# Inverse square roots of a two-stage convolution kernel: GpSimd's power in place of ScalarE seeds and VectorE Newton steps

## The reference

```
x = x + L0(gn(x), mask)                       # x: 8 x 64 x 16 x 16, fp32
x = x + L1(gn(x), weight, alphas, betas, bias)
gn: 32 groups of 2 channels: (g - mean(g)) / sqrt(var(g) + 1e-5)

L0, contextual attention, per image (f = gn(x)):
  fd = f[:, ::2, ::2]                         # 8 x 8 positions
  w  = 3x3 patches of fd;  wn = w / max(|w|, 1e-4)
  yi = <patches of fd, wn>                    # 64 x 64 cosines
  yi = fuse(fuse(yi) turned) turned back      # two 3-tap diagonal sums
  yi = softmax(10 * yi * mm, over patches) * mm   # mm: patches clear of the mask
  out = transposed conv of yi with 4x4 patches of f / 4
L1: 3x3 convolution 64 -> 64; its weight is w*a / (1 + exp(w*b)) in 4 x 4 blocks, plus bias
```

## Time and profile before

| | |
|---|---|
| Time, median of 3 runs | 55.9 us (55.76 to 56.01) |
| Span of the profiled execution | 53.4 us, first to last instruction |
| Time around that span | 55.9 - 53.4 = 2.5 us (the profiled execution has no separate time but its span) |
| PE busy | 39.2 us, 73%, 502 matmuls |
| DVE busy | 34.8 us, 65%, 143 instructions |
| ACT busy | 16.0 us, 30%, 50 instructions |
| POOL busy | 19.5 us, 37%, 49 instructions |
| ACT, the Ln of the group norms | 4 instructions, mean 204 ns |
| DMA | 2.37 MB, mean 44 GB/s |

### The profile page before, as it was taken

How to read it: one execution, slowest core, us unless ns; L and a number is a source line. 1 busy time by engine, 2 the same in 40 slices (tenths; PEclk the granted TensorE clock), 3 DMA queues, 4 the chain that set the end, 5 groups by cost and what they waited for, 6 DMA issues and landing times.

```text
span 53.4 us, 1316 instructions
## 1 busy us (share of the span) xinstructions
PE 39.2 (73%) x502; PEld 25.6 (48%) x502; DVE 34.8 (65%) x143; ACT 16.0 (30%) x50; POOL 19.5 (37%) x49
## 2 busy tenths in 40 slices
PE   1996757996999988999589908999999999000000
PEld 0331242673389876986369704444468886000000
DVE  3907799769896889999999999959990200300000
ACT  4500304666752352726798420004300000000000
POOL 5994887979999600203006960000000000000000
PEclk9999999999999999999999999999999999999555
DMA  0399996000000000000000000000000111111110
GB/s 0 88 370 228 310 184 140 5 0 0 18 0 0 0 0 0 12 0 0 0 12 0 0 0 0 0 0 0 0 0 18 37 42 48 49 48 49 48 49 18
DMA packets 2335, 2.37 MB, mean 44 GB/s; under 512 B 281, under 2 KB 2201, under 8 KB 2330
## 3 DMA queue, kind: packets, MB, share of 16 engines
q1 hardware_dynamic: 1770, 1.96, 14.3%
q10 hardware_dynamic: 560, 0.33, 2.0%
HBM read 1.77 MB, written 0.52 MB: 43 GB/s over the span
## 4 chain that ended last, share of the span: by engine, by line
DVE 42%; PE 30%; DMA 6%; issue 3%; ACT 3%; DVEq 0%
PE bank L583 12%; PE bank L595 12%; DMA xh<-x_in_dram 6%; DVE gn_stats L674 4%; DVE wrec L761 3%; PE bank L488 3%; DVE x2h L704 2%; DVE fst L704 2%; DVE ftl L822 2%; DVE pst L807 2%; DVE x L830 2%; DVE xn L704 2%; DVE n2c L774 2%; DVE p L807 1%; DVE gn_mv L678 1%
## 5 line engine op out<-in xcount | busy, mean ns | idle before, releaser
L478 PE MATMUL bank<-idle 128*128 128x512 f16 x27 | 8.7, 455 | 1.1 <-POOL idle L278 1.1
L305 POOL TENSOR_SCALAR fq<-xh,gn_mean,gn_rstd 128x128 f32<-128x128 f32 x8 | 6.7, 852 | 0.2 <-DVE xn L704 0.2
L488 PE MATMUL bank<-fmv,fst 128*64 128x128 f16 x108 | 4.2, 224 | 1.0 <-ACT fmv L381 0.8
L921 DVE SCALAR_TENSOR_TENSOR o_sb<-bank,x1b 128x256 f32<-128x256 f32 x4 | 1.6, 422 | 5.0 <-PE bank L595 5.0
L543 PE MATMUL bank<-k_sb,pst 128*64 128x256 f16 (+2 forms) x72 | 4.3, 262 | 0.8 <-DVE pst L713 0.7
L488 PEld LDWEIGHTS bank<-fmv,fst 128*64 128x64 f16 x108 | 3.3, 108 | 2.8 <-ACT fmv L381 2.8
L478 PEld LDWEIGHTS bank<-idle 128*128 128x128 f16 x27 | 2.7, 116 | 4.2 <-issue 1.8
L337 POOL TENSOR_TENSOR wl<-w,wh 64x288 f16<-64x288 f32 x4 | 2.9, 726 | 3.6 <-ACT wh L457 3.4
L543 PEld LDWEIGHTS bank<-k_sb,pst 128*64 128x64 f16 x72 | 3.3, 109 | 1.5 <-DVE pst L713 0.8
L360 ACT ACTIVATE gn_ln<-gn_var 128x2 f32<-128x2 f32 x4 | 0.8, 204 | 9.6 <-DVE gn_var L687 9.5
L583 PE MATMUL bank<-x2h,wh 128*128 128x512 f16 x9 | 2.4, 388 | 1.6 <-DVE x2h L704 1.6
(11 more groups left out here) (120 smaller groups left out, 90.7 us busy)
## 6 DMA issues: line engine op xcount, KB each, us to landing
xg<-x_in_dram SPq DMA_DIRECT2D x2, 256.0 KB, 6.2
out_dram<-o_sb SPq DMA_DIRECT2D x4, 128.0 KB
k_sb<-k_dram SPq DMA_DIRECT2D x1, 496.0 KB, 5.8
xh<-x_in_dram SPq DMA_DIRECT2D x1, 256.0 KB, 3.2
xh<-x_in_dram ACTq DMA_DIRECT2D x1, 256.0 KB, 3.6
w_sb<-weight_in_dram SPq DMA_DIRECT2D x1, 72.0 KB, 2.9
c_sb<-c_dram ACTq DMA_DIRECT2D x1, 64.0 KB, 3.0
c_sb<-c_dram SPq DMA_DIRECT2D x1, 64.0 KB, 5.9
```

What stands on the lines that cost most here:

```text
L305: pool.tensor_scalar(fq[u][:, j, 2 * q:2 * q + 2, :].rearrange("p s (a b) -> p s a b", a=G), xh[u][:, j, :].rearrange("p (a r b s) -> p r ...
L478: te.matmul(ps, idle[:, 0:P], idle[:, :], start=True, stop=True)
L488: i = te.matmul(gram_ps[u][half(g), :, :], st, mv[:, :, k // 3:k // 3 + G, k % 3:k % 3 + G], start=part_st == part_mv == k == 0, stop=part ...
```

## The change

ScalarE's seeds and VectorE's Newton steps go. In their place GpSimd raises the 128x2 tile to the power -0.5 in one tensor_tensor instruction, with a tile `power` that it fills once. `F_SCALE` and `Y_SCALE` become 1, since the result of the power is used as it is. VectorE then waits for `rstd_ready` or `rnorm_ready` from GpSimd. The six powers are put at fixed places in GpSimd's program.

```diff
-F_SCALE = 16.0
-Y_SCALE = 16.0
+F_SCALE = 1.0
+Y_SCALE = 1.0
...
@@ gpsimd
+            def gn_rstd(i, u):
+                n = norm[i][u]
+                pool.wait_ge(var_ready, UNITS * i + u + 1)
+                pool.tensor_tensor(n.rstd[:, :], n.var[:, :], power[:, :], ALU.pow).then_inc(rstd_ready, 1)
+
+            def inverse_norms(u):
+                pool.wait_ge(n2_ready, u + 1)
+                pool.tensor_tensor(rnorm[u][:, :], n2c[u][:, :], power[:, :], ALU.pow).then_inc(rnorm_ready, 1)
+
             zero([idle], idle_set)
+            link(pool.memset(power[:, :], -0.5))
...
             zero(pst, zeros_p)
+            gn_rstd(0, 0)
             zero([wh, wl], zeros_w)
             pool.wait_ge(mask_in, 16)
...
+            gn_rstd(0, 1)
             pool.wait_ge(xn_ready, 1)
             f_by_parity(0, 0)
+            inverse_norms(0)
...
             for j in range(IPU):
                 f_by_parity(1, j)
+            inverse_norms(1)
             zero(x2h + x2l, zeros_x2)
...
             pool.wait_ge(zeros_x2, 2 * UNITS)
+            gn_rstd(1, 0)
+            pool.wait_ge(rstd_ready, UNITS + 1)
             for g in range(2):
...
+            pool.wait_ge(wl_ready, 4)
+            gn_rstd(1, 1)
@@ scalar
-                link(act.activation(scratch[:, :], v[:, :], ACT.Ln, scale=1.0 / scale ** 2))
-                return act.activation(y[:, :], scratch[:, :], ACT.Exp, scale=-0.5)
...
@@ vector
-            def newton(dst, v, y, a, b, scale):
-
-                link(dve.tensor_tensor(a[:, :], y[:, :], y[:, :], ALU.mult))
-                link(dve.scalar_tensor_tensor(b[:, :], a[:, :], -0.5 / scale ** 2, v[:, :], ALU.mult, ALU.mult))
-                return dve.scalar_tensor_tensor(dst[:, :], b[:, :], 1.5, y[:, :], ALU.add, ALU.mult)
-
             def gn_rstd(i, u):
-                n = norm[i][u]
-                dve.wait_ge(gn_y0, UNITS * i + u + 1)
-                link(newton(n.rstd, n.var, n.y0, n.ya, n.yb, F_SCALE))
+                dve.wait_ge(rstd_ready, UNITS * i + u + 1)
...
             def high_x2(u):
...
+                gn_rstd(1, u)
+                for r in range(2):
+                    copy_x1(u, 1, r)
                 dve.wait_ge(zeros_x2, 2 * UNITS)
```

More of the change, by code:

```diff
@@ L136, in __init__ @@
                 self.var = sb(name + "_var", P, IPU)
[L137 to L140, removed]
                 self.rstd = sb(name + "_rstd", P, IPU)
@@ L150, in build @@
         gdiag = per_unit("gdiag", P, IPU, L)
-        n2, n2c, nln, ny0, nya, nyb, rnorm = (per_unit(t, P, IPU) for t in (
-            "n2", "n2c", "nln", "ny0", "nya", "nyb", "rnorm"))
+        n2, n2c, rnorm = (per_unit(t, P, IPU) for t in ("n2", "n2c", "rnorm"))
+        power = sb("power", P, IPU)
         y32 = per_unit("y32", P, IPU, L)
@@ L189, in build @@
         idle_set = sem("idle_set")
-        pool_step, dve_step, act_step = map(sem, ("pool_step", "dve_step", "act_step"))
+        pool_step, dve_step = map(sem, ("pool_step", "dve_step"))
         mask_row, mask_bc, keep_ready = map(sem, ("mask_row", "mask_bc", "keep_ready"))
@@ L193, in build @@
         wexp_ready, w32_ready, wh_ready, wl_ready = map(sem, ("wexp_ready", "w32_ready", "wh_ready", "wl_ready"))
-        moments, groups, var_ready, mean_ready, gn_y0 = map(sem, (
-            "moments", "groups", "var_ready", "mean_ready", "gn_y0"))
+        moments, groups, var_ready, mean_ready, rstd_ready = map(sem, (
+            "moments", "groups", "var_ready", "mean_ready", "rstd_ready"))
         xn_ready, fh_center, fl_center, fq_ready = map(sem, ("xn_ready", "fh_center", "fl_center", "fq_ready"))
         f_copied = [[sem(f"f_copied{u}{part}") for part in range(2)] for u in range(UNITS)]
-        gram_done, n2_ready, norm_y0, y32_ready, yh_ready, yl_ready = map(sem, (
-            "gram_done", "n2_ready", "norm_y0", "y32_ready", "yh_ready", "yl_ready"))
+        gram_done, n2_ready, y32_ready, yh_ready, yl_ready = map(sem, (
+            "gram_done", "n2_ready", "y32_ready", "yh_ready", "yl_ready"))
         rnorm_ready = sem("rnorm_ready")
@@ L348, in _ @@
             act.dma_start(par_sb[:, :], par).then_inc(par_in, 16)
[L350 to L358, removed]
-                link(act.activation(scratch[:, :], v[:, :], ACT.Ln, scale=1.0 / scale ** 2))
-                return act.activation(y[:, :], scratch[:, :], ACT.Exp, scale=-0.5)
-            def gn_seed(i, u):
-                n = norm[i][u]
-                act.wait_ge(var_ready, UNITS * i + u + 1)
-                seed(n.y0, n.var, n.ln, F_SCALE).then_inc(gn_y0, 1)
             def exp_weight(b):
@@ L386, in weight_alpha @@
                                scale=par_sb[:, b:b + 1]).then_inc(walpha_ready, 1)
-            def norm_seed(u):
-                act.wait_ge(n2_ready, u + 1)
-                seed(ny0[u], n2c[u], nln[u], Y_SCALE / F_SCALE).then_inc(norm_y0, 1)
             def high_y1(u):
@@ L421, in _ @@
             act.wait_ge(zeros_f, 2 * UNITS)
-            gn_seed(0, 0)
             copies_of_f(0, 0)
             copies_of_f(0, 1)
-            gn_seed(0, 1)
             act.wait_ge(w_in, 16)
@@ L430, in _ @@
             copies_of_f(1, 0)
-            norm_seed(0)
             copies_of_f(1, 1)
@@ L438, in _ @@
             high_y1(0)
-            norm_seed(1)
             act.wait_ge(zeros_p, UNITS)
@@ L458, in _ @@
                                    ACT.Copy).then_inc(wh_ready, 1)
-            gn_seed(1, 0)
             high_b(1)
             x1_and_bias(0)
-            gn_seed(1, 1)
             x1_and_bias(1)
@@ L774, in norms @@
                 dve.tensor_scalar(n2c[u][:, :], n2[u][:, :], MIN_NORM2, None, ALU.max).then_inc(n2_ready, 1)
-            def inverse_norms(u):
-                dve.wait_ge(norm_y0, u + 1)
-                newton(rnorm[u], n2c[u], ny0[u], nya[u], nyb[u], Y_SCALE / F_SCALE).then_inc(rnorm_ready, 1)
             def normalise_gram(u):
@@ L868, in _ @@
             low_f(1)
-            inverse_norms(0)
             normalise_gram(0)
@@ L880, in _ @@
             logits(0)
-            inverse_norms(1)
             normalise_gram(1)
```

## The result

The changed kernel takes 57.36 us (57.31 to 57.78, 4 runs) against 55.83 us (55.73 to 56.01, 4 runs): a ratio of 1.0294, interval 1.0255 to 1.0333. It is slower, by 1.5 us. The profiled execution took 57.36 us with a span of 55.5 us.

What follows compares the result with a forecast made beforehand. VectorE's chain, then TensorE's convolution, was taken to bound the kernel. A delay of 2.0 less a gain of 0.6 made the 53.4 us span 54.8; with 2.5 around it, 57.3 us, 8-in-10 range 55.8 to 61.8.

Steps and rivals of the forecast that it cites:

- Scale costs nothing: F and Y at scale 1 change constants and no instruction, so they cost 0.
- c = 0.6: What one power costs GpSimd's queue, from release to hand-over: 0.6 us, between ends of 0.3 and 0.84.
- the delay: Unit 1's patch norms: the power, queued behind other GpSimd work, ends at 21.27, so yh(1) starts 2.0 us later.
- Hidden powers: Powers for unit 0's first group norm and patch norms finish while VectorE is busy, so VectorE does not wait.
- Second norm, unit 0, 1.3 at x2h: Without the slow Newton steps, the x2h pair ends at 30.8 instead of 32.07, 1.3 us gained for the convolution's start.
- The second wait, 0.6 kept: VectorE's x2 pair meets wl, TensorE waits for unit 1's statistics, and 0.6 of the 1.3 us gained stays.
- Second norm, unit 1, at 0: Its power waits for wl, two copies cover most of it, and TensorE still has unit 0's matmuls: cost 0.
- The end moves one for one with the convolution's start: TensorE is busy 13.15 of 13.20 us from 32.20, so the end follows the convolution's start unless a wait opens.
- 2.5 us around the span: The median lies 2.5 us above the profiled span, and the same distance was assumed after the change.
- GpSimd's queue without a gap: Sign: GpSimd's queue runs without idle from 6.1 us until the second rnorm at about 21.3.
- The slow power: Rival: a power computed element by element in software may take 2 us or more, giving 64.3 us; chance 0.15.
- the draw: Rival: a power costs 0.3 us and the gain is near 0.9, giving 55.8 us; chance 0.08.

Runs made afterwards that it cites:

- e1: The kernel before with F_SCALE and Y_SCALE at 1 and nothing else changed: 55.78 us, ratio 0.9994.
- e4: The changed kernel with a multiply of the tile `power` by itself in place of each power, same queue places and waits: 54.90 us.
- e6: The changed kernel with GpSimd's first power moved behind the two memsets and three mask operations: 54.98 us.
- e2: The kernel before at scale 1, with GpSimd's power in the second group norm only: 55.56 us.
- e8: The changed kernel with GpSimd's four wl subtractions held back until x2 of unit 0 is written: 57.19 us.
- e12: The changed kernel with GpSimd's queue and unit 1's transposes reordered, two idle matmuls out, wl after x2, stores from two queues: 54.43 us.
- e7: The changed kernel with the power of unit 1's norms moved ahead of its last two fq in GpSimd's queue: 57.07 us.
- e5: The changed kernel with each power computed twice, the first into a spare tile: 61.89 us.

## Why the prediction was right

57.36 against 57.3. The mechanism held: four powers and all that stands between them in GpSimd's queue, less a part won back in the second group norm. That the total fits to 0.1 us is luck: errors of 0.4 to 0.7 cancel in points 2 and 8.

1. *Scale costs nothing*: e1, 0.9994.
2. *c = 0.6.* The 0.6 was a choice between the ends 0.3 and 0.84, which came from instructions of other kinds; no run shows how GpSimd works out a power, only its price. A power is 0.70 busy (a multiply 0.19, e4), and its four places in the queue cost 2.79 us together (6.36 to 6.99, 12.31 to 13.04, 14.70 to 15.39, 20.71 to yh(1) at 21.45) where 2.4 was said. The work between them took 12.30 instead of 12.76, mostly the wden and fq at 5.32 for 5.64, and the first power started 0.25 later. So 21.27 came out as 21.45, the delay as 2.01 for 2.0. The form of the term was right (four powers and all that is queued between), and e4 and e6 show both halves of it, price and order. Its size was right by two errors of 0.4 and 0.5 in opposite directions.
3. *Hidden powers*: (0,0) and rnorm(0) hold up nobody on VectorE, as said. The first nevertheless costs its 0.63 in the queue behind it.
4. *Second norm, unit 0, 1.3 at x2h.* The pair ends at 33.30; before's 32.07 and the 2.18 by which yh(1) is later make 34.25, so 0.95 was gained. The third copy waits 0.30 for the power, which I had put exactly at the copies' end: a term of 0 that was 0.3.
5. *The second wait, 0.6 kept.* The x2 pair is blocked as said (1.14, free 0.72), the aggregates end at 36.58, 0.53 earlier than 34.93 + 2.18, TensorE waits 0.30, and 0.54 stays. e2 repeats it alone, e8 shows the pairs unblocked.
6. *Second norm, unit 1, at 0.* Its copies wait 0.28 for the power (38.47). Nothing shows of it here, but in e8 this wait was 0.80 and ate the gain: the cover was thinner than I said.
7. *The end moves one for one with the convolution's start.* Incomplete. In all fourteen traces the span ends 13.7 to 14.3 us after the first store is issued (before 13.69, after 14.02), while from the last o_sb it is 8.0 to 9.5. So the end follows the o_sb of unit 0 more closely; they stand in VectorE's queue behind unit 1's x2l. That is read from the traces and was not tested by itself. Here both moved nearly alike (first store +1.77, last o_sb +1.64), so the step gave the right number. In e12 it would not have: there the last o_sb is 2.3 earlier than before (43.10), the first store 1.3, the median 1.4.
8. *2.5 us around the span.* 1.86 here. Kernels without ScalarE's seeds have 1.7 to 2.0 in their timed runs, those with them 2.05 to 2.4 (e2 twice 1.9); my 2.5 set a median against the span of another execution. The span itself was 0.7 above the forecast (0.46 tail, 0.17 start, 0.06 less gain), and that hid it. Why the distance differs is open.

Of the signs that were named, GpSimd's queue without a gap and both waits are there, but their sizes differ. The wait before high_f(1) is 2.73 and not about 1, although high_f(1) itself is late by 1.34 only (beyond x): the 1.15 of ScalarE's seed and the Newton steps that stood there before has become waiting. The wait before yh(1) is 1.57 for 2. The convolution starts at 33.45 for 32.9 and waits 0.30 for 0.6, by point 4 and the later x. The slope of 0.45 us for each 0.1 of c is a little low by the prediction's own ends (57.3 to 58.5 for 0.24, so 0.5).

The slow power, the draw and the cheap power are out: 0.70 us lies in the range in which none decides. The draw's ground, that two elements cost no more than any small instruction does, holds for the multiply (0.19) and not for the power.

## What to carry to other kernels

When work moves from a waited-for engine to an idle one, walk the receiver's queue: what counts is what stands before each moved instruction and what it now holds up, not the engine's busy share (here 42%). Put a new instruction behind work that could run while its input is not ready, and check what its neighbours, shifted in turn, will collide with. Look for the transfer that the end hangs on before calling the last compute engine the bound.

## What the runs showed of the hardware

- A GpSimd power of 128x2 takes 0.70 us, a multiply of the same shape 0.19.
- Back-to-back GpSimd memsets held up a VectorE fp16 copy until the last had ended: 1.05 us beside the memsets of x2h and x2l (four, 0.37 each), 0.20 alone (e7).
- The output stores move 48 GB/s on about 2.2 DMA engines, while the inputs reached 352 GB/s in one of the page's 40 slices. Each store's pattern begins with a dimension of 2 (`g` in the rearrangement). The Trainium skill, "DMA: Bandwidth & Descriptors", section "Why a DMA increments its semaphore by 16 and not by 1", says that a DMA uses as many engines as the largest number up to 16 that divides the slowest dimension of both its patterns; with 2 here and the 128 partitions of o_sb that is 2. The trace agrees: the share reads 1.10 and 1.11 of 16 engines at 6 to 8 us of the kernel before, when the inputs keep all of them busy, so two busy engines would read as 2.2, by estimate. A store with a longer first dimension was not tried, and might shorten the tail of some 14 us that no kernel here touched.
- TensorE fell to the 1.2 GHz level after a wait of 2.81 us (e5), and in the profile of e8 after one of 1.92 (its row is below). The longest wait alone doesn't tell: e7 kept a granted clock of 1.00 after 1.66 us at the same place, and of two kernels with much the same waits at the start the changed one fell by 8 us (0.97 and 0.83) and e6 didn't (0.79 and 0.83).

```profile
16.00:21.00 5.00, 5.00 (x75) 4.58 (x76) 2.53 (x14) 1.22 (x4) 4.89 (x7) 0.50 0.00 0
```
